# Shared-key attention: who scales the probabilities, and how far the transposes trail the scores

## The reference, cut to what matters

```python
Q = jnp.einsum('bnd,hdk->bhnk', x, proj_q)
K = jnp.einsum('bmd,dk->bmk', x, proj_k)
V = jnp.einsum('bmd,dv->bmv', x, proj_v)
logits = jnp.einsum('bhnk,bmk->bhnm', Q, K)
weights = jax.nn.softmax(logits, axis=-1)
O = jnp.einsum('bhnm,bmv->bhnv', weights, V)
Y = jnp.einsum('bhnv,hdv->bnd', O, proj_o)
```

## Time and profile before

| what | value |
|---|---|
| time, median of 3 runs | 982.57 us (980.1 to 984.23) |
| the profiled execution's own time | 984.73 us |
| its span in the trace | 982.3 us |
| PE busy | 889.5 us (91%) |
| DVE busy | 668.3 us (68%) |
| ACT busy | 500.9 us (51%) |
| POOL busy | 334.9 us (34%) |
| the stage's loop, first scores to the next stage's transposes | 510.62 to 684.10 us |

### The profile page before, as it was taken

How to read it: one execution, slowest core, us unless ns; L and a number is a source line. 1 busy time by engine, 2 the same in 40 slices (tenths; PEclk the granted TensorE clock), 3 DMA queues, 4 the chain that set the end, 5 groups by cost and what they waited for, 6 DMA issues and landing times. The chain is left out here.

```text
span 982.3 us, 13451 instructions
## 1 busy us (share of the span) xinstructions
PE 889.5 (91%) x4332; PEld 488.0 (50%) x4332; DVE 668.3 (68%) x1371; ACT 500.9 (51%) x996; POOL 334.9 (34%) x340
## 2 busy tenths in 40 slices
PE   5889988999999998599999999998989999769996
PEld 2445553433333324366667888787433322534575
DVE  4865667888889944435558776875699896455654
ACT  3786544677777773012126656563207778243321
POOL 7335636400000001136557666563420000125833
PEclk9999998999999999699989999999998999959999
DMA  5030017122212810753240000000200550075200
GB/s 157 1 139 22 1 31 117 24 51 51 48 43 53 297 54 1 261 232 126 87 129 1 1 1 1 1 1 1 81 3 20 194 196 1 1 281 181 70 17 27
DMA packets 41656, 73.81 MB, mean 75 GB/s; under 512 B 8964, under 2 KB 27780, under 8 KB 40436
## 3 DMA queue, kind: packets, MB, share of 16 engines
q1 hardware_dynamic: 36372, 59.68, 19.9%
q0 software_dynamic: 4400, 13.11, 4.3%
q10 hardware_dynamic: 816, 0.17, 0.1%
HBM read 49.67 MB, written 10.49 MB: 61 GB/s over the span
## 5 line engine op out<-in xcount | busy, mean ns | idle before, releaser
L1081 DVE TENSOR_REDUCE c_amx<-PS 128x1 f32<-128x512 f32 x256 | 159.1, 683 | 27.5 <-PE PS L981 27.1
L1174 ACT ACTIVATE c_aE<-PS 128x512 f32<-128x512 f32 x256 | 132.6, 602 | 47.1 <-PE PS L993 46.9
L1881 POOL TENSOR_SCALAR s_Pn<-s_Pr,s_rs 128x512 f32<-128x512 f32 x64 | 100.4, 1569 | 55.7 <-DVE s_rs L1923 55.6
L72 POOL TENSOR_SCALAR rstd<-mv 128x4 f32<-128x4 f32 x8 | 1.9, 234 | 336.6 <-DVE mv L95 336.6
L981 PE MATMUL PS<-c_aKs,c_aQs 99*128 99x512 bf16 x256 | 96.4, 387 | 5.1 <-DMA c_aQs<-area 3.6
L993 PE MATMUL PS<-c_aQs,c_aKs 99*128 99x512 bf16 x256 | 94.5, 380 | 3.5 <-ACT c_aE L1174 2.3
L1081 DVE TENSOR_REDUCE h_amx<-PS 128x1 f32<-128x512 f32 x128 | 79.5, 682 | 8.7 <-PE PS L981 8.3
L1174 ACT ACTIVATE h_aE<-PS 128x512 f32<-128x512 f32 x128 | 67.6, 600 | 21.6 <-PE PS L993 21.3
L2019 ACT ACTIVATE s_Pr<-PS,s_nmx 128x512 f32<-128x512 f32 x64 | 44.2, 690 | 65.5 <-DVE s_nmx L1916 65.5
L1004 PE MATMUL PS<-c_aE,c_VB 128*17 128x512 f32 x512 | 67.4, 598 | 0.1
L981 PEld LDWEIGHTS PS<-c_aKs,c_aQs 99*128 99x128 bf16 x256 | 24.9, 98 | 79.0 <-DVE c_amx L1081 55.4
(11 more groups left out here) (486 smaller groups left out, 1969.7 us busy)
## 6 DMA issues: line engine op xcount, KB each, us to landing
area<-in_e_w SPq DMA_DIRECT2D x16, 512.0 KB, 10.1
area<-in_g_w SPq DMA_DIRECT2D x8, 1024.0 KB, 6.3
c_aKs<-area SPq DMA_DIRECT2D x48, 128.0 KB
g_B<-in_g_b SPq DMA_DIRECT2D x1, 4096.0 KB, 14.1
c_aQs<-area SPq DMA_DIRECT2D x48, 64.0 KB
h_aQs<-h_QP SPq DMA_DIRECT2D x48, 64.0 KB
early<-in_ctxT SPq DMA_DIRECT2D x2, 1024.0 KB, 7.6
e_B<-in_e_b SPq DMA_DIRECT2D x1, 2048.0 KB
```

What stands on the lines that cost most here:

```text
L1081: dve.tensor_reduce(self.mx[:, qt, j, half:half + 1], PS[:, n % MB, :], AX.X, ALU.max).then_inc(self.max_done, 1)
L1174: act.activation(self.E[kt % 2][:, j, :], PS[:, MB + x % XB, :], ACT.Exp, scale=0.25).then_inc(self.exp_done, 1)
L1881: pool.tensor_scalar(Pn[g % NPB][:, :], Pr[g % NPB][:, :], rs[:, g % NPB:g % NPB + 1], None, ALU.mult).then_inc(pn_ready, 1)
```

## The change

POOL's loop over the tiles goes; only the layer-norm helper for the next stage is left there. DVE takes the same instruction, directly behind the reciprocal that it needs, so its `inverse_sum(g - 1)` now also writes `s_Pn` of tile g - 1. DVE waits for its own reciprocal in between, and for the transposes that last read the buffer. LAG is 2 instead of 3: transposes, output, projection and the evacuations that belong to them come one step earlier against the scores, the loop has 76 steps instead of 77, and there are 4 buffers instead of 5 of `Pr`, `Pn` and the row statistics. The last quarter of a unit's output then falls into qt 2, `take_o` to the end of ACT's list of that step, `low_output` to the head of DVE's list in qt 3, and the first quarter of the next unit's output into qt 3.

```diff
-    LAG = 3
+    LAG = 2
...
-            for g in range(G):
-                pool.wait_ge(rs_ready, g + 1)
-                if g >= NPB:
-                    pool.wait_ge(t_mm, g - NPB + 1)
-                pool.tensor_scalar(Pn[g % NPB][:, :], Pr[g % NPB][:, :], rs[:, g % NPB:g % NPB + 1], None,
-                                   ALU.mult).then_inc(pn_ready, 1)
-                if g == G - TB:
-                    following.gpsimd(pool, range(1))
+            following.gpsimd(pool, range(1))
             following.gpsimd(pool, range(1, B))
...
                 dve.reciprocal(rs[:, g % NPB:g % NPB + 1], sm[:, g % NPB:g % NPB + 1]).then_inc(rs_ready, 1)
+                dve.wait_ge(rs_ready, g + 1)
+                if g >= NPB:
+                    dve.wait_ge(t_mm, g - NPB + 1)
+                dve.tensor_scalar(Pn[g % NPB][:, :], Pr[g % NPB][:, :], rs[:, g % NPB:g % NPB + 1], None,
+                                  ALU.mult).then_inc(pn_ready, 1)
```

## The result

| | before | after |
|---|---|---|
| median, us | 983.40 (4 runs, 980.1 to 985.03) | 999.63 (4 runs, 999.0 to 1000.02) |
| ratio | | 1.0164, interval 1.0141 to 1.0187 |
| profiled execution: time, span | 984.73, 982.3 | 999.0, 997.2 |
| loop (first scores to the next stage's first transposes) | 173.48 | 189.29 |
| unit in the middle | 10.15 | 11.23 |

The change makes the kernel slower by 16.2 us. The loop alone is longer by 15.81, so the cost lies in it; what lies before and behind it differs, taken together, by 0.9 us between the two traces.

What follows compares the result with a forecast made beforehand. PE was taken to bound the middle of the loop, at 10.15 us a unit. The terms summed to +20.0 us, 1004.7 for the profiled execution and 1002.6 against the median, range 1000 to 1005.5 at 0.70.

Steps and rivals of the forecast that it cites:

- The stall: At qt 2, PE waits 1.28 us once a unit for the bank of the next unit's first output.
- signs of being wrong: Units staying at 10.2 us, PE's waits ending on `s_Pn`, or the loop's granted clock falling below 1.00.
- The mis-sized term: Price of the 128x512 scaling on DVE: 0.68 us, slot 0.60, extrapolated from rows at 128 and 256 columns.
- rival 1: Scaling on DVE runs at the cast's rate, slot 0.33: +13.7, 996.3 us; chance 0.13.
- The upper end: Highest price for the scaling on DVE: 0.855 us, the mean of a 128x512 product of two SBUF tensors.
- The chain: DVE's list at qt 2, from maximum through scaling, `s_PTl` and `s_QT..l` to `s_OT..l`; PE starts at 4.52, wanted at 3.24.
- unit 1: Second unit of the loop, set by DVE alone: 11.36 against 7.59 us, +3.8.
- ten units in the middle: Units 4 to 14 except the one with the first batch's output: ten times 1.28, +12.8 us.
- The tail: Unit 15 to the next stage: 1.50 of one step and 1.4 of POOL waits go, chain gives some back: -1.1 us.
- Rival 2: Scaling hides and only the new order costs: 0.72 a unit, +6.6, 989 us; chance 0.05.
- Rival 3: Scaling takes 0.855, slot 0.78, and DVE's step no longer fits PE's short step: +24, 1007 us; chance 0.07.
- Rival 4: PE stays the bound since DVE fits by sums (10.12 of 10.15): +1.2, 983.8 us; chance 0.05.

Runs made afterwards that it cites:

- e4: Changed kernel without any scaling, the transposes reading the exponentials as they are; median 988.98 us, ratio 1.0060 to the kernel before.
- e5: Changed kernel with the low output formed without reading bank 5, so the next output waits only for ACT's copy; median 994.71 us, ratio 1.0121 to the kernel before.
- e3: Changed kernel with a second scaling of the same tile into a spare tile, before the one that counts; median 1011.47 us, ratio 1.0272 to the kernel before.
- e6: Changed kernel with the scaling's per-partition factor replaced by the constant 0.5; median 997.66 us, ratio 1.0152 to the kernel before.
- e7: Changed kernel plus 27 scalings on DVE behind the loop, differing in columns and number of per-partition factors; 1009.54 us, a single execution.
- e9: Changed kernel with the scaling on DVE put behind the low transposes and LAG 4; median 987.80 us, ratio 1.0051 to the kernel before.
- e8: Changed kernel with the scaling on DVE put behind the low transposes and LAG 3; median 990.04 us, ratio 1.0071 to the kernel before.
- e1: Changed kernel with LAG 3 instead of 2, the scaling still on DVE; median 995.73 us, ratio 1.0127 to the kernel before.

## Why the prediction was right

**Direction and mechanism: right.** The forecast was +20.0 us, 1002.6; measured are +16.2 and 999.63. The stall stands where it was put: once a unit, in front of the first output product, behind `s_QT..l` and `s_OT..l` on DVE, with the wait for `s_PTl` inside it. e4 and e5 show that PE waits for the low output in its earlier step, e3 and e6 that one scaling a unit is in the chain. None of the prediction's signs of being wrong came: the middle unit is 11.23, its waits end on `s_OT..l`, and the granted clock stays at 1.00.

**The mis-sized term: the scaling.** It was taken at 0.68 with a slot of 0.60, and took 0.487 with a slot of 0.41 (579.63 to 580.04). The fault is in the slope. The rows at 256 and at 128 columns have two factors and one, and the difference of 0.122 was read as the price of 128 columns. By e7 it is 0.065 for the columns and 0.06 for the second factor; 0.286 + 3 x 0.065 = 0.481 would have been the price. It lies nearer to the cast of rival 1 than to the value taken. (The upper end, 0.855, was no plain duration either: it is the mean of eight whose median is 0.692.) The Trainium skill's page "VectorE: DVE Perf Modes", section on the perf-mode tier table, gives this operation two elements a cycle, and the prediction doubted it by those rows. e7 bears the page out on the rate: 1536 more columns than 512 at 0.065 per 128 give an estimate of 0.417 + 0.78 = 1.20 us at 2048, where the page has 1227 ns. No run here has 2048 columns, and the price of a factor was told by the runs alone.

**The chain with that one number replaced.** Forecast: `s_PTl` at 2.49, `s_QT..l` 3.08, `s_OT..l` 3.68, PE at 4.52. Measured from 577.73: 2.31, 2.91, 3.51, PE at 4.33. Everything but the scaling's slot was right to 0.02, and the stall is 4.33 - 3.24 = 1.09 where 1.28 was forecast.

**The sum by its terms, us:**

| term | forecast | measured |
|---|---|---|
| unit 0 | +0.3 | +0.5 |
| unit 1 | +3.8 | +2.9 |
| unit 2 | +1.3 | +1.2 |
| unit 3 | +1.1 | +0.9 |
| ten units in the middle | +12.8 | +10.7 |
| unit with batch 0's output | +1.8 | +1.3 |
| last unit and tail | -1.1 | -1.7 |
| together | +20.0 | +15.8 |

Ten times 0.19 of chain are 1.9 of the 2.1 missing in the middle. In unit 1, which DVE's sum sets, four slots shorter by 0.2 explain 0.8 of the 0.9. So 2.7 of the 4.2 us that are missing are that one term, and the units 3 and with batch 0's output hold the same shorter chain.

**The tail: a term misread.** The forecast's -1.1 counts 1.4 us of waits for POOL that end. The prediction put both of these waits near the end, but one, 1.02, is at 525.92, in unit 1, and only 0.42 is in the tail, at 669.16; at both places PE's own wait ended on `s_PTl`. Without this term the forecast would have been +0.3. What made up for it: the chain's 1.3 did not come in the last unit, where PE waits for 0.19 us before 683.29 and 0.70 before 685.28, and three waits of the last unit before went (0.46 before 661.07, 0.25 before 669.19, 0.72 before 670.54). That the tail came out within 0.6 of its forecast is luck.

**The rivals.** Rival 1 is half true: the rate is that of the cast, but the factor's 0.06 us is on top, and the result lies between the two. Rival 2 (only the order costs) gave 0.72 a unit and 989; e4, which has the order without the scaling, took 0.72 a unit and 988.98. So its price was right, with ACT's copy as the cause, and its claim that the scaling hides was wrong. Rival 3 falls with the duration. Rival 4 (PE stays the bound) did not happen here, but its argument that DVE has room was right, with the list written otherwise and LAG 4: e9.

**Not foreseen** were that the halves do not add up (10.8, or 9.3 at full clock, and 11.2 against 15.8), and the second late start that e5 uncovered.

## What to carry to other kernels

An engine's spare time over a loop (here 2.87 of 10.15 us) does not say that an instruction fits: find what the next engine waits for soonest after it, and put the new instruction behind that in the list (e8 against e1: some 3.6 us of loop at full clock, for the same work). To shorten a lag between two stages, first count which other instructions it brings into the same step; here that moved `low_output` and cost 0.72 us a unit without any scaling. A duration extrapolated from two rows needs rows that differ in one thing only.

## What the runs showed of the hardware

- A `TENSOR_SCALAR` on DVE from SBUF to SBUF in float32 costs about 0.16 us and 0.065 per 128 columns, and a per-partition factor a fixed 0.06 on top: 417, 476 and 537 ns at 512 columns with none, one and two (e7; the last with a second operation too), 426 against 487 in the loop (e6).
- The granted clock fell to 0.50, the level of 1.2 GHz, inside the loop of three profiled executions, each time behind an idle PE: 2.13 us in front of 631.00 in e1, 1.72 in front of 528.23 in e3, 1.27 and 0.94 in front of 522.34 in e6. It was back at 1.00 by 636 in e1, 536 in e3 and 526 in e6. In the kernel after the loop has waits of 1.45 us at 634.02 and of 1.33 and 1.00 at the front, and its clock stays at 1.00. The length of the wait alone does not decide: e3 also waits for 2.21 us in front of 644.31, e9 for 1.95 in front of 628.31, and their clock stays at 1.00 there. What does decide is open.
- The same scaling took 1.569 us on POOL, 3.2 times as long as on DVE.
